# Rotary embedding of the queries: the halves are exchanged by two DMAs of a VectorE product instead of by ScalarE copies

## What is computed

```python
def rope(t, offset=0):
    ...
    t1, t2 = (t[..., :d // 2], t[..., d // 2:])
    return jnp.concatenate([t1 * cos - t2 * sin, t2 * cos + t1 * sin], axis=-1)
...
q = (x @ Wq.T).reshape(b, n, H, D)
...
q = rope(q)
k = rope(k)
scores = jnp.einsum('bnhd,bmhd->bhnm', q, k) * scale
...
p = jax.nn.softmax(scores, axis=-1)
o = jnp.einsum('bhnm,bmhd->bnhd', p, v).reshape(b, n, H * D)
return o @ Wout.T
```

## Time and profile before

| | us |
|---|---|
| median of 3 runs | 885.23 |
| lowest and highest | 879.88, 886.64 |
| the profiled execution, its device time | 881.3 |
| its span, first to last instruction | 879.5 |
| attention loop, from L555 of body 1 to L555 of body 60 | 505.2 |

### The profile page before, as it was taken

The page is one execution under the profiler, slowest core; times in us unless marked ns, Lnnn a source line. Parts: engine busy times, 40 slices in busy tenths (PEclk is TensorE's granted clock), DMA queues, the critical chain, the costliest instruction groups (busy, mean ns, idle before and its releaser), DMA issues.

```text
span 879.5 us, 13251 instructions
## 1 busy us (share of the span) xinstructions
PE 777.1 (88%) x4016; PEld 626.1 (71%) x4016; DVE 568.3 (65%) x1535; ACT 514.8 (59%) x1168; POOL 553.3 (63%) x455
## 2 busy tenths in 40 slices
PE   4758988999889999989999989998992999999784
PEld 3646767778678888768888768886671788887563
DVE  6636666667767777777777677876641276663347
ACT  2637666777676767776676767676620355542142
POOL 1458888888587887678877677782055433324751
PEclk9978999999999999999999999999996999999877
DMA  9022133532122221212221212110322334412321
GB/s 310 30 85 68 59 113 119 154 97 64 48 59 63 73 73 61 61 49 73 67 68 61 66 55 58 64 61 25 127 74 77 104 135 177 177 73 79 100 80 60
DMA packets 42898, 75.76 MB, mean 86 GB/s; under 512 B 5712, under 2 KB 19408, under 8 KB 42832
## 3 DMA queue, kind: packets, MB, share of 16 engines
q1 hardware_dynamic: 38944, 65.52, 23.1%
q0 software_dynamic: 3072, 8.39, 3.0%
q10 hardware_dynamic: 816, 1.05, 0.4%
HBM read 57.77 MB, written 17.17 MB: 85 GB/s over the span
## 4 chain that ended last, share of the span: by engine, by line
PE 55%; POOL 16%; DVE 11%; ACT 9%; issue 6%; another core or an unknown queue 2%; DMA 1%; ACTq 0%; DVEq 0%; POOLq 0%
PE ps L343 17%; PE ps L845 9%; PE ps L813 8%; PE ps L859 6%; PE ps L831 5%; PE ps L965 4%; ACT prob L546 3%; POOL q_sw L1529 3%; POOL q_sw L1524 3%; POOL kh_row L1538 3%; POOL o_lo L1543 3%; ACT o_hi L574 1%; DVE ps L1169 1%; DVE stats L1213 1%
## 5 line engine op out<-in xcount | busy, mean ns | idle before, releaser
L546 ACT ACTIVATE prob<-ps,neg_max 128x512 f32<-128x512 f32 (+3 forms) x256 | 132.5, 526 | 77.5 <-DVE neg_max L1169 77.4
L845 PE MATMUL ps<-pt,vp 128*128 128x512 f32 (+3 forms) x512 | 148.8, 433 | 1.5 <-DVE pt L1182 1.5
L1533 POOL TENSOR_TENSOR q_lo<-q_sw,q_hi 128x512 fp32r<-128x512 f32 x64 | 85.8, 1341 | 63.0 <-ACT q_hi L568 63.0
L845 PEld LDWEIGHTS ps<-pt,vp 128*128 128x128 f32 x512 | 82.6, 190 | 49.6 <-issue 16.6
L1161 DVE TENSOR_TENSOR q_cos<-ps,rope_sb 128x512 f32<-128x512 f32 x64 | 44.2, 691 | 113.9 <-ACT q_sw L535 113.9
L1169 DVE CUSTOM_DVE_ANT_0 ps<-ps,causal_row 128x512 f32<-128x512 f32 (+3 forms) x256 | 117.3, 519 | 0.0
L1543 POOL TENSOR_TENSOR o_lo<-o_t,o_hi 128x512 fp32r<-128x512 f32 x64 | 82.2, 1284 | 55.6 <-ACT o_hi L574 55.3
L831 PE MATMUL ps<-id_f,prob 128*128 128x128 f32 x640 | 94.8, 280 | 14.2 <-ACT pt L555 14.2
L813 PE MATMUL ps<-k_hi,q_hi 128*128 128x512 f32 (+3 forms) x256 | 91.3, 357 | 7.4 <-ACT prob L546 3.6
L831 PEld LDWEIGHTS ps<-id_f,prob 128*128 128x128 f32 x640 | 75.0, 143 | 25.2 <-issue 16.9
L1524 POOL TENSOR_TENSOR q_sw<-q_sw,rope_sb 128x512 f32<-128x512 f32 x64 | 82.2, 1284 | 10.2 <-ACT q_sw L535 10.2
(11 more groups left out here) (200 smaller groups left out, 1917.6 us busy)
## 6 DMA issues: line engine op xcount, KB each, us to landing
kh_row<-kvh_rows SPq DMA_DIRECT2D x64, 256.0 KB, 3.1
inv_row<-inverse_sums SPq DMA_DIRECT2D x64, 256.0 KB, 3.1
slot_inputs<-zeros SPq DMA_DIRECT2D x8, 640.0 KB, 4.8
xg<-slot_inputs SPq DMA_DIRECT2D x8, 640.0 KB, 4.6
slot_outputs<-yo SPq DMA_DIRECT2D x8, 640.0 KB, 3.4
up_raw<-in_w_up_dram SPq DMA_DIRECT2D x8, 368.0 KB, 4.7
x_sb<-in_x_dram SPq DMA_DIRECT2D x4, 512.0 KB, 8.9
wo_raw<-in_wout_dram SPq DMA_DIRECT2D x4, 512.0 KB, 8.1
```

The costliest lines, as they stand in the source:

```text
L546: ins = act.activation(prob[:, i % 2, ROW_AT[nt]:ROW_AT[nt] + w], ps_s[bank][:, at:at + w], ACT.Exp, scale=-1.0, bias=neg_max[:, i % 2, nt ...
L845: ins = pe.matmul(ps_qo[:, mt * P:SEQ], vp[:, b * TPB + mt, :], pt[:, i % 2, cols], start=(mt == 0), stop=(mt == PT_BANKS[-1][-1]))
```

## The change

The product with the sine is taken before the exchange instead of after it. VectorE writes `q_turn = -(q * sin_sb)` (one instruction that multiplies by -1 and by the table, since the sine has opposite signs in the two halves), and ScalarE then issues two DMAs of 64 partitions by 2 KB each that bring its halves crosswise into `q_sw`. ScalarE's two copies and GpSimd's `sin_q` are gone. `rotate` waits for both DMAs. `cos_q` waits for the queries themselves, for the last unit's DMAs and for the last unit's sum. `o_t` gets two buffers, which lie where `o_lo` lies.

```diff
-                act.wait_ge(q_psum, i + 1)
+                act.wait_ge(q_turned, i + 1)
                 act.wait_ge(q_ready, i) if i else act.wait_ge(kt_ready, B)
-                act.copy(q_sw[0:64, :], ps_qo[64:128, :])
-                act.copy(q_sw[64:128, :], ps_qo[0:64, :]).then_inc(q_swapped, 1)
+                act.dma_start(q_sw[0:64, :], q_turn[64:128, :]).then_inc(q_swapped, 16)
+                act.dma_start(q_sw[64:128, :], q_turn[0:64, :]).then_inc(q_swapped, 16)
...
             def cos_q(i):
-                dve.wait_ge(q_swapped, i + 1)
+                dve.wait_ge(q_psum, i + 1)
+                if i:
+                    dve.wait_ge(q_swapped, 32 * i)
+                    dve.wait_ge(q_sum_ready, i)
+                else:
+                    dve.wait_ge(kt_ready, B)
+                dve.scalar_tensor_tensor(q_turn[:], ps_qo[:], -1.0, sin_sb, ALU.mult, ALU.mult).then_inc(q_turned, 1)
                 dve.tensor_tensor(q_cos[:], ps_qo[:], cos_sb, ALU.mult).then_inc(q_cos_ready, 1)
...
                 dve.wait_ge(inv_row_in[i % 2], 16 * (i // 2 + 1))
-                if i:
-                    dve.wait_ge(o_lo_ready, i)
-                dve.tensor_tensor(o_t[:], ps_qo[:], inv_row[:, i % 2, :], ALU.mult).then_inc(o_ready, 1)
+                if i >= 2:
+                    dve.wait_ge(proj_psum, i - 1)
+                dve.tensor_tensor(o_t[:, i % 2, :], ps_qo[:], inv_row[:, i % 2, :], ALU.mult).then_inc(o_ready, 1)
...
-            def sin_q(i):
-                pool.wait_ge(q_swapped, i + 1)
-                pool.tensor_tensor(q_sw[:], q_sw[:], sin_sb, ALU.mult).then_inc(q_sin_ready, 1)
-
             def rotate(i):
                 pool.wait_ge(q_cos_ready, i + 1)
-                pool.wait_ge(q_sin_ready, i + 1)
+                pool.wait_ge(q_swapped, 32 * (i + 1))
                 pool.tensor_tensor(q_sw[:], q_cos[:], q_sw[:], ALU.add).then_inc(q_sum_ready, 1)
```

More of the change, by code:

```diff
@@ L130, in decoder_layer @@
         prob = place("prob", R2 + 48 * KB, [2, PACKED])
-        inv_row = place("inv_row", R2 + 58 * KB, [2, SEQ])
-        o_t = place("o_t", R2 + 62 * KB, [SEQ])
+        inv_row = place("inv_row", R2 + 60 * KB, [2, SEQ])
+        q_turn = place("q_turn", R2 + 58 * KB, [SEQ])
         o_hi = place("o_hi", R2 + 64 * KB, [2, SEQ], F32R)
         o_lo = place("o_lo", R2 + 68 * KB, [2, SEQ], F32R)
+        o_t = place("o_t", R2 + 68 * KB, [2, SEQ])
         pt = place("pt", PT_AT, [2, PACKED])
@@ L246, in decoder_layer @@
             sem("wq_hi_ready"), sem("wq_ready"), sem("wo_hi_ready"), sem("wo_ready"))
-        q_psum, q_swapped, q_cos_ready, q_sin_ready, q_sum_ready, q_hi_ready, q_ready = (
-            sem("q_psum"), sem("q_swapped"), sem("q_cos_ready"), sem("q_sin_ready"), sem("q_sum_ready"),
+        q_psum, q_swapped, q_cos_ready, q_turned, q_sum_ready, q_hi_ready, q_ready = (
+            sem("q_psum"), sem("q_swapped"), sem("q_cos_ready"), sem("q_turned"), sem("q_sum_ready"),
             sem("q_hi_ready"), sem("q_ready"))
@@ L573, in head_of_output @@
                     act.wait_ge(proj_psum, i - 1)
-                act.copy(o_hi[:, i % 2, :], o_t[:]).then_inc(o_hi_ready, 1)
+                act.copy(o_hi[:, i % 2, :], o_t[:, i % 2, :]).then_inc(o_hi_ready, 1)
             def copy_gathered(b):
@@ L789, in queries @@
                 if i:
-                    pe.wait_ge(q_swapped, i)
+                    pe.wait_ge(q_turned, i)
                     pe.wait_ge(q_cos_ready, i)
@@ L835, in weigh_values @@
                 n = min(i + 4, UNITS)
-                pe.wait_ge(q_swapped, n)
+                pe.wait_ge(q_turned, n)
                 pe.wait_ge(q_cos_ready, n)
@@ L1542, in rest_of_output @@
                 pool.wait_ge(o_hi_ready, i + 1)
-                pool.tensor_tensor(o_lo[:, i % 2, :], o_t[:], o_hi[:, i % 2, :].bitcast(F32), ALU.subtract) \
+                pool.tensor_tensor(o_lo[:, i % 2, :], o_t[:, i % 2, :], o_hi[:, i % 2, :].bitcast(F32), ALU.subtract) \
                     .then_inc(o_lo_ready, 1)
@@ L1551, in _ @@
             pool.wait_ge(kt_ready, B)
-            sin_q(0)
             rotate(0)
@@ L1555, in _ @@
             rest_of_queries(0)
-            sin_q(1)
             rotate(1)
@@ L1561, in _ @@
             scale_keys(2)
-            sin_q(2)
             rotate(2)
@@ L1577, in _ @@
                 if i + 3 < UNITS:
-                    sin_q(i + 3)
                     rotate(i + 3)
```

## The result

The changed kernel takes 917.26 us at the median (907.42 to 918.05, 4 runs) against 883.22 for the one before (879.88 to 886.64, 4 runs): ratio 1.036, 95% interval 1.0275 to 1.0444. It is slower by 3.6%. The forecast was 876 us, in a range of 865 to 890, and slower had a chance of 0.20. The profiled execution took 917.02, span 915.2, so the span is 35.7 us longer than before, and that is what has to be explained.

What follows compares the result with a forecast made beforehand. TensorE was taken to bound 34 laps, GpSimd's chain 16 laps and the sequence ends. Terms +0.5, -8.4, -5.2 and +6.0 gave -7.1, 874.2 against 881.3; set against the four-run mean, 876 us, range 865 to 890.

Steps and rivals of the forecast that it cites:

- The bounds before: Attention loop: TensorE alone bounds 34 laps (7.91 us each in bodies 21 to 33); GpSimd and ScalarE bound bodies 1 to 17.
- The path in front of L556: ScalarE, old L555: queries, VectorE's product, two issues, L555, group 2, queries; lap 8.08 us, 0.17 over TensorE's own.
- the price of the two issues: ScalarE's two DMA issues before old L555: taken as 0.81 us, between 0.62 and 1.00.
- the lap of 8.08: Attention loop: 0.04 + 0.69 + 0.03 + 0.81 + 0.02 + 6.49 us, forecast to bound 34 laps and 16 more.
- the 34 laps: Laps TensorE bounded before: forecast at 8.08 us each, 274.7 against 268.7, +6.0 us.
- the sum: Whole kernel: all terms together -7.1 us, 874.2 against the profiled 881.3.
- The 16 laps: Stretch from 83.89 to 222.61, held by GpSimd before: forecast at 130.3 us against 138.72, -8.4.
- The sequence ends: Three stretches where a sequence ends: 1.38 us from GpSimd and 1.20 - 0.83 from ScalarE, -1.7 each, -5.2.
- The start: From the start to L555 of body 1: first three rotations wait for transfers, ScalarE gets back 0.4; +0.5 us in all.
- C: Rival: transfers land late, from 3.1 us the landing sets the lap; at 3.5, +12.4, about 896 us; chance 0.18.
- D: Rival: issues before old L555 are dear, a pair at 1.00 makes the lap 8.27; +2.4, 886 us; chance 0.17.

## Why the prediction was wrong, point by point

**The bounds before** were read rightly. GpSimd's lap after 83.89, TensorE's after 255.55 and GpSimd's part in the sequence ends are confirmed by the version without the sine product, which gained 10.8 and 4.6 us there and nothing in the laps that TensorE bounded.

**The path in front of L556** was named as the step that decides, and it did. The product is 0.70 (put at 0.69), the gaps on either side of it are 0.02 and 0.03 (put at 0.04 and 0.03), the part from L556 to the queries is 312.67 - 306.14 = 6.53 (put at 6.49).

**The failed step is the price of the two issues**: 0.81, with 1.00 as the upper bound, against 1.11 measured, and 0.11 instead of 0.02 from there to L556. It was taken from a pair of SyncE's loads of rows from DRAM, and the bound from ScalarE's first two DMAs, also from DRAM. No row had a transfer from SBUF to SBUF, so neither was a bound. Stores with their source in SBUF did not settle it either: in the trace before they are 0.34 and 0.54 each.

```profile
45.94 0.34 SPq L369 DMA_DIRECT2D kvh_rows<-hc_t  x1
...
309.12 0.54 SPq L381 DMA_DIRECT2D inverse_sums<-inv_t  x1
```

The 0.30 and 0.09 missing there, and 0.03 net in the other pieces, turn the lap of 8.08 into the measured 8.50. Over the 34 laps that is 110.50 + 110.80 + 67.99 = 289.3 instead of the 274.7 of the sum, 14.6 us. The 16 laps take 138.81 instead of 130.3, another 8.5, of which 6.7 is the lap of 8.50; the rest lies in the five longer laps, for which the sum had 1.0. That is 23 of the 43 us between the sum's -7.1 and the +35.7 that came.

**The sequence ends** were put at -1.7 each. They came at -0.2, +1.7 and 0.0, 6.7 us off in all. The sum had credited them with what ScalarE saves; the chain at 231 to 263 us passes VectorE's product twice, with issues behind it, and the ends got 2 to 5 us shorter when SyncE issued. How the 6.7 us divide is not shown.

**The start** was put at +0.5 and came at +8.2, 7.7 off. The first landing took 5.4 us, issued behind the key rows and a 704 KB load; a landing of 2.3 had been used for it. This was a second mis-sized term, of which the version on SyncE shows 3.0 us; the other 5 were not taken apart. In the trace before, key rows landed after 5.2 us at the most and 3.1 at the median, which pointed to a range for it.

**After body 60** 5.4 us more were spent, of which 1.1 in the last laps and 4.3 after attention, where nothing was changed. There the kernels of this study took 270 to 277 us with no order that follows their changes; the granted clock from L556 of body 63 to the end was 0.91, against 0.92 before. I count it as scatter and did not settle it.

**The rivals.** C, the late landing, was the one on the right side (it gave about 896), and it was not what set the laps of 8.50: with an eighth of the bytes they stayed. It has a part in the five longer laps at 92 to 231 us. D was right in kind, dear issues, but its price ended at 1.00, so it forecast "no change". Left open upward to two of the dearest stores, 1.08, with 5 us for a late start, the range would have ended at 883.3 - 7.1 + 50 x 0.27 + 5 = about 895, still short. The transfers were indeed next in line, as C had it: once the issues were off the path, laps of 8.1 to 8.5 on the mean appeared, with landings of 4.2 in the chain.

## What to carry to other kernels

A copy that is replaced by a DMA isn't gone from the engine that issues it: here two issues and the gap behind them took 1.22 us of ScalarE where two copies had taken 1.20. Price the issue from a row with the same kind of source and target, and if none exists, don't close the range upward. Where an issue must wait for another engine's result, look at who stands behind it in that stream; here the order of two lines, or another queue, was worth more than the whole change (894.67 and 880.43 against 917.26). And before an exchange of partitions is sent through a queue, see whether the engine that makes the product can write it to the other half: that version took 867.13.

## What the runs showed of the hardware

All these are medians. An issue of a DMA from SBUF to SBUF held ScalarE's queue 0.47 us, alone or first, over 64 or 128 partitions, with 2 KB or 256 bytes a partition, and SyncE's 0.49; a second one right behind it took 0.60 to 0.62, and 0.53 with an instruction between them. Loads of a row from DRAM to all partitions took 0.31 to 0.32 in the same kernel. Landing took 1.9 us for 16 KB, 2.4 for 128 KB (64 partitions) and 2.6 for 256 KB (128 partitions), each from its own issue, and up to 5.5 in single cases beside other transfers. The Trainium skill (SBUF — State Buffer, "Can I just issue two DMAs to hit both halves?") has two transfers of 64 partitions serialize; here the second of a pair landed 2.4 us after its own issue, the first 2.3 after its own, and a single one, in the version with one issue, after 2.3 too. The estimate in the prediction by that page was 2.9 for the second, which this trace does not bear out at this size; whether the two wait for each other over a larger transfer no run here shows. VectorE wrote the product of one half of a bank into the other 64 partitions in 0.69 us, the time of all 128.
